# Three late stores issued as nine row-strided transfers each, in a streaming cross-network kernel

## The reference: what is computed

```
def step(x, wb):
    wi, bi = wb
    xw = jnp.matmul(x, wi)          # one number per row
    x_new = x0 * xw + bi + x
    return (x_new, None)
x, _ = jax.lax.scan(step, inputs, (w, b))
```

## Time and profile before

| what | value |
|---|---|
| median of three runs | 1279.35 us (1278.41 to 1281.69) |
| the profiled execution: its time | 1279.0 us |
| its span, first to last instruction | 1277.3 us |
| DVE busy | 1167.0 us (91%) |
| PE busy | 790.4 us (62%) |
| DMA traffic | 537.74 MB, mean 421 GB/s |
| DMA traffic in most slices | 427 to 433 GB/s |
| DMA traffic in the last two slices of 40 | 412 and 172 GB/s |

### The profile page before, as it was taken

One profiled execution on the slowest core, in us unless ns is written; L12 is line 12 of the kernel. 1 busy time (PEld: TensorE's weight loads), 2 busy tenths in 40 slices (PEclk: granted clock), 3 DMA queues, 4 the chain that ended last, 5 costly groups with the idle time before them and its releaser, 6 DMA issues.

```text
span 1277.3 us, 22775 instructions
## 1 busy us (share of the span) xinstructions
PE 790.4 (62%) x10394; PEld 739.8 (58%) x10394; DVE 1167.0 (91%) x652; ACT 109.5 (9%) x390; POOL 4.3 (0%) x17
## 2 busy tenths in 40 slices
PE   7677666666556556656566556565666457676661
PEld 3666656656456556556566556565565457675561
DVE  5999999998898988989989889899999999999893
ACT  2000000000000000000000000000000011111110
POOL 1000000000000000000000000000000000000000
PEclk9777787777877877877777787777777877778766
DMA  9999999999999999999999999999999999999994
GB/s 369 427 399 432 430 431 432 431 431 430 432 430 433 428 433 429 432 429 432 431 432 430 431 430 431 432 431 431 431 431 430 431 428 429 428 427 428 427 412 172
DMA packets 37480, 537.74 MB, mean 421 GB/s; under 512 B 4192, under 2 KB 4192, under 8 KB 4800
## 3 DMA queue, kind: packets, MB, share of 16 engines
q1 hardware_dynamic: 37296, 536.89, 98.7%
q10 hardware_dynamic: 144, 0.30, 0.1%
HBM read 268.73 MB, written 268.44 MB: 421 GB/s over the span
## 4 chain that ended last, share of the span: by engine, by line
DMA 58%; DVE 33%; issue 4%; PE 2%; SPq 1%; ACTq 0%; ACT 0%; DVEq 0%
DMA tiles<-in_r_inputs_dram 48%; DVE tiles L285 17%; DVE blocks L261 16%; DMA out_dram<-tiles 9%; DMA tiles<-in_L_rec_b_dram 1%; PE dots L363 1%; SPq L155 1%; DVE scale L273 0%; PE strips L353 0%; PE dots L405 0%; ACTq L202 0%; PE scratch L343 0%; ACT spread L219 0%; PE turned L374 0%; DVEq L48 0%
## 5 line engine op out<-in xcount | busy, mean ns | idle before, releaser
L405 PE MATMUL dots<-blocks,weights 128*64 128x128 f32 x6528 | 554.7, 349 | 308.6 <-DVE blocks L261 308.5
L405 PEld LDWEIGHTS dots<-blocks,weights 128*64 128x64 f32 x6528 | 526.6, 185 | 329.0 <-DVE blocks L261 328.8
L261 DVE STREAM_TRANSPOSE blocks<-tiles 128x2048 f32<-128x2048 f32 x256 | 576.1, 2288 | 76.5 <-issue 65.5
L285 DVE SCALAR_TENSOR_TENSOR tiles<-tiles,scale,c_low 128x2048 f32<-128x2048 f32 x129 | 299.1, 2319 | 0.9
L285 DVE SCALAR_TENSOR_TENSOR tiles<-tiles,scale,scratch 128x2048 f32<-128x2048 f32 x129 | 299.8, 2325 | 0.0
L363 PE MATMUL dots<-blocks,weights 128*64 128x64 f32 x3328 | 148.8, 273 | 52.4 <-DVE blocks L261 45.3
L363 PEld LDWEIGHTS dots<-blocks,weights 128*64 128x64 f32 x3328 | 144.9, 187 | 56.6 <-issue 56.4
L219 ACT ACTIVATE spread<-dots,group_mask 128x128 f32<-128x128 f32 (+1 forms) x308 | 82.3, 350 | 1038.8 <-PE dots L405 849.9
L374 PE MATMUL turned<-layer_sel,spread 128*128 128x8 f32 x512 | 71.0, 262 | 93.1 <-ACT spread L219 93.1
L374 PEld LDWEIGHTS turned<-layer_sel,spread 128*128 128x128 f32 x512 | 64.3, 194 | 109.3 <-issue 80.4
L229 ACT ACTIVATE growth<-turned,ones 128x16 f32<-128x16 f32 (+1 forms) x77 | 20.9, 271 | 81.9 <-PE turned L374 81.9
(11 more groups left out here) (24 smaller groups left out, 11.6 us busy)
## 6 DMA issues: line engine op xcount, KB each, us to landing
tiles<-in_r_inputs_dram SPq DMA_DIRECT2D x128, 2048.0 KB, 30.3
out_dram<-tiles SPq DMA_DIRECT2D x127, 2048.0 KB, 25.9
out_dram<-tiles SPq DMA_DIRECT2D x4, 512.0 KB, 7.0
tiles<-in_L_rec_w_dram ACTq DMA_DIRECT2D x1, 96.0 KB
tiles<-in_L_rec_b_dram ACTq DMA_DIRECT2D x4, 24.0 KB
tiles<-in_L_rec_b_dram ACTq DMA_DIRECT2D x1, 96.0 KB
```

The costliest lines, as they stand in the source:

```text
L261: nc.vector.transpose(blocks[:, p % PLACES, :], source).then_inc(blocks_ready, 1)
L285: done = nc.vector.scalar_tensor_tensor(out=tile[:, at], in0=tile[:, at], scalar=scale[:, u % 2, t, L - 1:L], in1=c, op0=ALU.mult, op1=ALU ...
L405: last = nc.tensor.matmul(dots[at:at + KM * Q, :, :, :], weights[:, c * CH // Q + k:c * CH // Q + k + KM, :], place[:, :, k * Q:(k + KM) * Q],
```

## The change

The stores of tiles 121, 123 and 125 are no longer one transfer of 128 rows each but nine: transfer r takes rows r, r+9, r+18 and so on of the tile, from the partitions of the same numbers. Since 128 = 2 x 15 + 7 x 14, two of the nine have 15 rows and seven have 14. The bytes are the same, and so is every other transfer. Each of the nine raises the place's semaphore by 16, so waits on such a place count 144 for such a tile; `stored_by` works that out.

```diff
+STEP = 9
+IN_NINE = (121, 123, 125)
...
+        def stored_by(n):
+            return sum(16 * STEP if m in IN_NINE else 16 for m in range(n % (TB * N_SLOTS), n + 1, TB * N_SLOTS))
...
                 sp.wait_ge(tiles_done, n + 1)
-                sp.dma_start(out_pairs[q, :, t, :], tiles[:, s, t, :]).then_inc(y_stored[s][t], 16)
+                if n in IN_NINE:
+                    for r in range(STEP):
+                        sp.dma_start(out_pairs[q, r:P:STEP, t, :],
+                                     tiles[r:P:STEP, s, t, :]).then_inc(y_stored[s][t], 16)
+                else:
+                    sp.dma_start(out_pairs[q, :, t, :], tiles[:, s, t, :]).then_inc(y_stored[s][t], 16)
...
-                    sp.wait_ge(y_stored[s][t], 16 * (q // N_SLOTS))
+                    sp.wait_ge(y_stored[s][t], stored_by(into - TB * N_SLOTS))
...
-                last_stores = 1 if n < n_tiles - 1 else STORE_PARTS
-                sp.wait_ge(y_stored[s][t], 16 * (q // N_SLOTS + last_stores))
+                more = 0 if n < n_tiles - 1 else STORE_PARTS - 1
+                sp.wait_ge(y_stored[s][t], stored_by(n) + 16 * more)
```

## The result

The changed kernel took 1286.89 us (median of 17 runs, 1282.96 to 1293.75), the kernel before 1279.38 us (17 runs, 1278.36 to 1283.13). The ratio is 1.0061 with a 95% interval of 1.0050 to 1.0071: 7.5 us slower by the medians, where 1.8 us slower was forecast. The profiled execution took 1287.65 us with a span of 1285.9 us, 8.6 us above's 1277.3.

A forecast was written before the change was run, and what follows sets the result against it. The late DMA engine's store backlog sets the end. Extra rows +1.8 to +1.9 us, completions 0.1, stepped reading 0.1, issues and waits 0 sum to +2.0 us: forecast 1281.2 us, range 1278.3 to 1286.0 us.

The forecast's parts named there:

- What bounds the kernel: At the program's end: one DMA engine's backlog of stores, about 14 us behind the other fifteen, and nothing else.
- Which engine it is: In the nine narrow stores of a tile: the late engine is one of the fourteen that carry 9 rows instead of 8.
- Rival A: Late engine left out of the narrow stores: 1265.0 us, or 1268.4 us if it carries 2 rows; chance 0.17.
- Rows on the late engine: One row more in each of 3 tiles at 0.61 to 0.63 us, on the path that sets the end: +1.8 to +1.9 us.
- Completions: 8 more small packets per changed tile, 24 in all, on the late engine: 0.1 us taken, 1.5 us at most.
- Reading with a step of nine partitions: Changed stores reading every ninth partition: 0.1 us taken, 2.8 us at most, as the late engine is nearly alone in much of its backlog.
- SP's issues: 8 more store issues per changed tile on SP, nine at 0.85 us being 7.7 us, hidden by full engines: cost 0.
- The other engines end later by up to 1.8 us: The 15 engines besides the late one finish later by this much, well inside their 14 us lead: cost 0.
- Rival B: Each of 27 single-row transfers makes the late engine pause, for completion or neighbouring reads; 0.15 us each gives 1285.2 us; chance 0.16.

## Why the prediction was wrong, point by point

- *What bounds the kernel:* right. The end is the late engine's backlog in both kernels (share 0.06 at the end), and its row costs 0.61 us.
- *Which engine it is:* right. Nine parts of each changed tile land late, so it carries 9 rows for 8. Rival A is out: no stretch ended early.
- *Rows on the late engine, +1.8 to +1.9 us:* no run shows this term alone. Where rows do not collide, 20 of them took 12.1 us, 0.61 us each, so the size stands as an estimate. It is a quarter of the loss.
- *Completions, at most 1.5 us:* right to take little. Nine transfers by columns have as many completions and more packets, and all of it is 1.3 us by the medians, not certain.
- *Reading with a step of nine partitions, taken as 0.1 us, 2.8 us at the most:* **this step failed.** The high end came from the slowest slice of the stream. That is the first slice, which holds the start, and nearly all its traffic is in transfers of 128 rows, so it says nothing of a row that an engine reads from others' partitions. The step in itself is free (26 GB/s when the late engine is alone); what costs is another engine at work on those partitions. The measured price is what is left of the 7.5 us: 7.5 - 1.8 = 5.7 us, of which the columns run puts 1.3 us down to the number of transfers (2.2 at the upper end of its interval). Of the late engine's time at tile 125 it is seen directly: 10.2 us for nine rows that take 5.5. I also argued that the late engine is nearly alone in its backlog. It is for the profile before; the edit puts the other engines beside it.
- *SP's issues, no cost:* right in the result, wrong in size. I took 0.85 us each at most, and most took about 2 us. Nine held SP for 20.9 us, not 7.7. By columns the same delay cost at most the 1.3 us above. In the changed kernel the late issues also let the others work until 1276 us, and so lengthen the time in which rows can collide; how much of the 5.7 us that adds was not separated. With two transfers a tile, where SP was not held, the loss was 6.4 us.
- *The other engines end later by up to 1.8 us:* wrong; they ended about 13 us later. That alone was not on the path, but it removed the cover for the term above.
- *Rival B* had the place and one of its two causes (another engine reads neighbouring partitions), though the rows themselves last longer and the engine does not pause. It named 0.07 us per row as the point of decision; 5.7 us over 27 rows are 0.21 us each. Its chance, 0.16, was set down by a bound of 0.06 us taken from whole quarter stores, which are transfers of all 128 rows again. The range ended at 1286.0 us, 0.9 short. The sum of the prediction gives 1281.3 us and not 1281.2, which changes nothing.

## What to carry to other kernels

A narrow transfer is not a slice of a wide one. Here transfers of all 128 partitions read each row at full rate. Most of those over fewer rows gave rows to engines that carry other partitions in a whole store, and those rows, and the whole stores beside them, slowed down. If a store has to be cut, cut it by columns: for three tiles, nine pieces of 128 rows cost 1.3 us, nine of 14 or 15 rows 7.5. And take the bound of an unknown cost from a row in which its mechanism can act; a row of the undisturbed stream bounds nothing.

## What the runs showed of the hardware that was not expected

- Rows read from partitions that another engine is working on: 1.2 to 1.4 us instead of 0.6, and the other engine's rows slow down too (0.9 to 1.2 us). A load beside such stores took 37.9 us to landing instead of 34.7. Alone, the same stepped rows took 0.6 us.
- SP's issue of a transfer is not a fixed price: 0.33 us for a whole store in the kernel before, 0.8 us for tile 121's nine, 2.0 and 2.3 us on average for the later ones, and up to 9.9 us for one of the pieces by columns. Its cause was not tested.
- One DMA engine, the fifth in the order in which narrow transfers take them, falls behind the other fifteen steadily: in the landing records of the kernel before, the last part of a transfer lands 1 us behind the fifteenth at 94 us, 8 us at 646 us and 17 us at 1202 us. Alone at the end, it works 14 us longer. Why it falls behind is open.
